# A second buffer of gathered rows, earlier gathers, VectorE low halves and a rewritten start in a chain of four conditioned residual layers

## The reference

```
x = x + L0(x)   # weight of each entry: (cond @ W_dec + b_dec) -> U (256 x 30), U @ V; out = x @ (U V) + bias
x = x + L1(x)   # y = (x * style) @ weight.T * dcoef, clipped to +-256; style, dcoef from cond
x = x + L2(x)   # up(relu(down(x))) + x, with down and up weights scaled and shifted by cond
x = x + L3(x):
    h = ln(x, pw_g[id], pw_b[id]); h = ln(h, cp_g[c], cp_b[c])       # rows gathered by a token id (250) and a class (5)
    t = ln(x, tm_g[c], tm_b[c]);   s = ln(x, ms_g[m], ms_b[m])
    m, n, r = x + mlp_ln(three states of the entry)
    cat = [w0 h, w1 t, w2 m, w3 n, w4 r, w5 s]                        # w = softmax(aw)
    return ln(silu(cat @ W1 + b1) @ W2 + b2) * g + be
```

## Time and profile before

| | us |
|---|---|
| median of 3 runs | 519.87 (519.48 to 520.92) |
| the profiled execution | 522.03 |
| its span, first to last instruction | 520.2 |
| TensorE matmul busy | 486.5 (94%) |
| VectorE busy | 411.8 (79%) |
| GpSimd busy | 406.3 (78%) |
| ScalarE busy | 356.9 (69%) |
| mean granted clock of TensorE | 0.988 |

### The profile page before, as it was taken

One profiled execution on the slowest core, in us unless ns is written; L12 is line 12 of the kernel. 1 busy time (PEld: TensorE's weight loads), 2 busy tenths in 40 slices (PEclk: granted clock), 3 DMA queues, 4 the chain that ended last, 5 costly groups with the idle time before them and its releaser, 6 DMA issues.

```text
span 520.2 us, 9616 instructions
## 1 busy us (share of the span) xinstructions
PE 486.5 (94%) x3216; PEld 360.9 (69%) x3245; DVE 411.8 (79%) x701; ACT 356.9 (69%) x667; POOL 406.3 (78%) x380
## 2 busy tenths in 40 slices
PE   8888598999999999999999999999999999988993
PEld 4854455577768686868686877777777768677782
DVE  4977698678878888878887888787888788887753
ACT  4679557547667777777878777777777776657732
POOL 6737699989787979798888888898989887786501
PEclk9999799999999999999999999999999999999997
DMA  8995507324435171708070717253433424114102
GB/s 302 319 332 108 126 1 219 81 83 93 117 71 137 37 210 30 217 2 241 4 219 28 205 42 186 60 151 96 121 127 89 160 61 134 59 38 126 41 2 80
DMA packets 35118, 61.82 MB, mean 119 GB/s; under 512 B 5108, under 2 KB 17542, under 8 KB 34709
## 3 DMA queue, kind: packets, MB, share of 16 engines
q1 hardware_dynamic: 28788, 44.01, 30.6%
q0 software_dynamic: 5440, 16.87, 11.2%
q10 hardware_dynamic: 864, 0.61, 0.4%
HBM read 52.61 MB, written 8.87 MB: 118 GB/s over the span
## 4 chain that ended last, share of the span: by engine, by line
PE 74%; ACT 8%; DVE 7%; issue 5%; POOL 4%; DMA 1%; DVEq 0%; ACTq 0%; POOLq 0%
PE ps_d L966 10%; PE ps_c L916 9%; PE ps_c L918 9%; PE ps_c L917 9%; PE ps_d L980 5%; PE ps_a L994 4%; PE ps_b L916 3%; PE ps_b L917 3%; PE ps_b L918 3%; PE ps_b L1012 3%; PE ps_a L1006 2%; POOL pw_rows L1532 2%; PE ps_a L1012 2%; DMA set_wdec<-in_W_dec 1%; PE ps_b L935 1%
## 5 line engine op out<-in xcount | busy, mean ns | idle before, releaser
L1232 ACT ACTIVATE h<-h,nb_h,rstd_h 128x256 f32<-128x256 f32 x64 | 33.3, 591 | 41.1 <-POOL nb_h L1562 41.1
L966 PE MATMUL ps_d<-xm_t,l_w 128*128 128x512 f32 x128 | 59.6, 609 | 1.6 <-DVE h L1455 0.9
L1532 POOL DMA_INDIRECT pw_rows<-in_pw,gidx x40 | 39.0, 976 | 12.2 <-issue 12.2
L1577 POOL TENSOR_TENSOR h<-xhat,pw_rows 128x1024 f32<-128x1024 f32 x16 | 38.0, 2372 | 6.4 <-ACT xhat L1232 6.4
L966 PEld LDWEIGHTS ps_d<-xm_t,l_w 128*128 128x128 f32 x128 | 23.5, 193 | 26.6 <-issue 24.5
L1598 POOL TENSOR_TENSOR w_up<-w_up,ugub 128x1024 f32<-128x1024 f32 x16 | 39.0, 2436 | 1.3
L1582 POOL TENSOR_TENSOR h<-h,pw_rows 128x1024 f32<-128x1024 f32 x16 | 38.3, 2394 | 1.2
L1596 POOL TENSOR_TENSOR w_up<-up_rep,ugub 128x1024 f32<-128x1024 f32 x16 | 38.1, 2379 | 1.1 <-issue 0.9
L1608 POOL TENSOR_TENSOR x3be<-x,ln_gb 128x1024 f32<-128x1024 f32 x16 | 37.9, 2371 | 0.6 <-DVE y_out L1513 0.6
L916 PE MATMUL ps_b<-w_h,act_t_l 128*128 128x256 f32 x128 | 37.7, 294 | 0.4 <-DVE act_t_l L1477 0.4
L994 PE MATMUL ps_a<-act_dn,w_up 128*128 128x128 f32 x256 | 32.5, 281 | 5.9 <-ACT act_dn L1211 5.3
(11 more groups left out here) (264 smaller groups left out, 1610.0 us busy)
## 6 DMA issues: line engine op xcount, KB each, us to landing
ugub<-ugub_scratch SPq DMA_DIRECT2D x32, 512.0 KB
x_t<-in_x_t SPq DMA_DIRECT2D x16, 512.0 KB
out<-y_out SPq DMA_DIRECT2D x15, 512.0 KB
set_wdec<-in_W_dec SPq DMA_DIRECT2D x2, 1920.0 KB, 9.9
set_wdec<-in_int_W SPq DMA_DIRECT2D x1, 1536.0 KB, 10.7
set_wdec<-in_nets_rows SPq DMA_DIRECT2D x1, 1152.0 KB, 15.4
set_wdec<-in_nets_W SPq DMA_DIRECT2D x1, 768.0 KB, 6.1
pw_rows<-in_pw,gidx POOLq DMA_INDIRECT x40
```

Of the source, the lines that this page charges most:

```text
L966: m = eng.matmul(ps_l1[:, o, :], l1_w[:, k, o * P:(o + 1) * P], xm_t[:, k, :], start=k == 0, stop=k == KB - 1)
L1232: m = eng.activation(out[:, j, :], src[:, j, :], ACT.Identity, bias=nb[k][:, j:j + 1], scale=rstd[k][:, j:j + 1])
L1532: eng.indirect_dma_start(pw_rows[:, j, :], None, t["pw"], bass.IndirectOffsetOnAxis(ap=idx[:, j:j + 1], axis=0)).then_inc(s_pw[c.ring], 16)
L1577: eng.tensor_tensor(h1[:, :, :], xhat[:, :, :], pw_rows[:, :, 0:D], ALU.mult).then_inc(g_h1m, 1)
```

## The change

- `pw_rows` becomes two buffers, and `g_gather` of a chunk waits for `g_hadd` of two chunks before instead of one. The gather of chunk 1 is issued right behind that of chunk 0.
- `y_out` becomes one buffer instead of two; the last two chunks write into `xm_t` and `x1_even`, which are free by then. `store` stands earlier in SyncE's lists (lag 5, ahead of `load_up`, instead of 6 behind it).
- `act_th2` signals its first strip by itself (`a_th` counts 3 a chunk, not 2), and `g_tlow` waits for that one.
- The four low halves of the weights are made by VectorE: `v_w2low`, `v_w1xlow`, `v_w1tlow`, `v_w1mlow`.
- `act_u` of chunk 0 goes in two halves. Several tiles of the start lie in tiles of later stages, to make room.
- `WARM` goes from 77 matmuls in seven places to 45 in six, and the begin lists of all engines are rewritten. The loop's lists and the end lists of TensorE, ScalarE, VectorE and GpSimd stay as they were.

```diff
-        pw_rows = sb("pw_rows", [P, CT, 2 * D])
+        pw_rows = [sb(f"pw_rows{r}", [P, CT, 2 * D]) for r in range(2)]
...
-        y_out = [late(f"y_out{r}", [P, CT, D]) for r in range(2)]
+        y_out = late("y_out", [P, CT, D])
...
+        y_late = {NCH - 2: rows_in(xm_t), NCH - 1: rows_in(x1_even)}
...
-        WARM = ((z_pool, 1, ps_b, 0, 24), (c_ug, 1, ps_d, 0, 17), (v_dca, 1, ps_a, 0, 8), (v_row, 1, ps_c, 0, 5),
-                (v_cls, 1, ps_c, 1, 2), (v_row, 1, ps_c, 0, 15), (v_ub, 1, ps_b, 1, 6))
+        WARM = ((z_pool, 1, ps_b, 0, 24), (c_ug, 1, ps_d, 0, 10), (v_dca, 1, ps_a, 0, 6), (v_row, 1, ps_c, 0, 1),
+                (v_row, 1, ps_c, 0, 1), (v_ub, 1, ps_b, 1, 3))
...
+        def v_w1xlow(eng, c):
+            eng.wait_ge(c_w1, 2)
+            eng.tensor_tensor(w1_l[:, 4:6, :], w1x[:, :, :], w1_h[:, 4:6, :].bitcast(F32),
+                              ALU.subtract).then_inc(v_wlx, 1)
...
         def act_th2(eng, c):
...
-            wait(eng, a_th, 2 * c.n + 1)
+            wait(eng, a_th, 3 * c.n + 1)
             wait(eng, p_x1, c.n)
-            for lo in (0, RP, 2 * RP):
+            eng.activation(t_st[0:RK, :], t_f, ACT.Copy).then_inc(a_th, 1)
+            for lo in (RP, 2 * RP):
                 m = eng.activation(t_st[lo:lo + RK, :], t_f, ACT.Copy)
             m.then_inc(a_th, 1)
...
         def v_ynorm(eng, c):
...
-            wait(eng, s_store[c.ring], 16 * c.half)
+            if isinstance(c.n, int) and c.n in y_late:
+                wait(eng, p_l1, NCH)
+                wait(eng, v_x3t, NCH - 1)
+            else:
+                wait(eng, s_store[1 - c.ring], 16 * (c.half + c.ring))
...
         def g_gather(eng, c):
...
-            wait(eng, g_h1, c.n)
+            wait(eng, g_h1, c.n - 1)
+            wait(eng, s_pw[c.ring], 16 * CT * c.half)
...
         def g_tlow(eng, c):
-            wait(eng, a_th, 2 * c.n + 2)
+            wait(eng, a_th, 3 * c.n + 2)
...
@@ SyncE @@
-                      order=[(load_ids, 2), (load_shift, 3), (load_x, 0), (load_ub, 0), (load_up, 0), (store, 6)],
+                      order=[(load_ids, 2), (load_shift, 3), (load_x, 0), (load_ub, 0), (store, 5), (load_up, 0)],
...
@@ GpSimd @@
-                      begin=[(g_ones, 0), (g_init, 0), (g_gather, 0), (g_b2rows, 0), (g_tlow, 0), (g_style, 0),
+                      begin=[(g_ones, 0), (g_init, 0), (g_gather, 0), (g_gather, 1), (g_b2rows, 0), (g_tlow, 0),
```

More of the change, by code:

```diff
@@ L251, in conditioned_residuals @@
             ugb = side[:, D + P:D + P + 2 * D]
[L252 to L256, removed]
+            wsq = w_up[:, 0:KB, :]
+            style2 = w_up[:, KB, :].rearrange("p (k b) -> p k b", k=KB)
+            flat_x3 = x3_t[:, :, :].rearrange("p k n -> p (k n)")
+            dm = [flat_x3[:, n * KB * B:(n + 1) * KB * B].rearrange("p (k b) -> p k b", k=KB) for n in range(3)]
+            st_nr = flat_x3[0:64 + 32, 3 * KB * B:3 * KB * B + B]
+            ugub_row = dn_2[:, :, :].rearrange("p a n -> p (a n)")
         nets = ((w1_mem, mu, 0, MU), (w1_nr, st_nr, 0, 64), (w1_nr, st_nr, 64, 96))
@@ L260, in late @@
             return ctx.enter_context(nc.sbuf_tensor(name, shape, dt, side="right"))
-        y_out = [late(f"y_out{r}", [P, CT, D]) for r in range(2)]
+        y_out = late("y_out", [P, CT, D])
+        x3_t_l = late("x3_t_l", [P, KB, CH], F32R)
         act_t_h, act_t_l = (late(f"act_t_{e}", [P, KB, CH], F32R) for e in "hl")
@@ L271, in conditioned_residuals @@
         x3 = late("x3", [P, CT, D])
-        x3_t_h, x3_t_l = (late(f"x3_t_{e}", [P, KB, CH], F32R) for e in "hl")
+        x3_t_h = late("x3_t_h", [P, KB, CH], F32R)
         x1_t = [x1_even, late("x1_odd", [P, KB, CH])]
+        rows_in = lambda tile: tile[:, :, :].rearrange("p k (a d) -> p (k a) d", d=D)
+        y_late = {NCH - 2: rows_in(xm_t), NCH - 1: rows_in(x1_even)}
         x2_t = x1_t
@@ L402, in split_in_place, with y_tile @@
             link(eng.tensor_copy(p3, src))
+        def y_tile(c):
+            return y_late[c.n] if isinstance(c.n, int) and c.n in y_late else y_out
         v_link = chain(nc.vector, v_chain)
@@ L949, in pe_x1 @@
                 eng.wait_ge(c_v, 2)
-            wait(eng, a_th, 2 * c.n + 2)
+            wait(eng, a_th, 3 * c.n + 3)
             wait(eng, g_tl, c.n + 1)
@@ L1070, in pe_hht @@
             if ahead(c, 3):
-                wait(eng, a_th, 2 * (c.n + 3) + 1)
+                wait(eng, a_th, 3 * (c.n + 3) + 1)
             wait(eng, v_h, c.n + 1)
@@ L1270, in act_msh @@
                 eng.wait_ge(v_w1x, 1)
[L1271 to L1272 removed]
+                eng.wait_ge(v_wlt, 1)
+                eng.wait_ge(v_wlm, 1)
             wait(eng, v_ms, c.n + 1)
@@ L1330, in act_store @@
             eng.wait_ge(e_y, 2)
-            eng.dma_start(one(out_d, c)[:, KB:CT - 1], y_out[c.ring][:, KB:CT - 1, :]).then_inc(s_last, 16)
+            eng.dma_start(one(out_d, c)[:, KB:CT - 1], y_tile(c)[:, KB:CT - 1, :]).then_inc(s_last, 16)
         def act_ysquare(eng, c):
@@ L1354, in act_onehot @@
             wait(eng, s_idx[c.ring], 32 * (c.half + 1))
+            wait(eng, a_oh, c.n)
             eng.activation(oh_sq[:, :], idx_ch[c.ring][:, :], ACT.Square, bias=cls_neg[RP:RP + CLS, 0:1]).then_inc(a_sq, 1)
@@ L1576, in g_hmul @@
             wait(eng, p_hht, c.n)
-            eng.tensor_tensor(h1[:, :, :], xhat[:, :, :], pw_rows[:, :, 0:D], ALU.mult).then_inc(g_h1m, 1)
+            eng.tensor_tensor(h1[:, :, :], xhat[:, :, :], pw_rows[c.ring][:, :, 0:D], ALU.mult).then_inc(g_h1m, 1)
         def g_hadd(eng, c):
             eng.wait_ge(g_h1m, c.n + 1)
-            eng.tensor_tensor(h1[:, :, :], h1[:, :, :], pw_rows[:, :, D:2 * D], ALU.add).then_inc(g_h1, 1)
+            eng.tensor_tensor(h1[:, :, :], h1[:, :, :], pw_rows[c.ring][:, :, D:2 * D], ALU.add).then_inc(g_h1, 1)
         def g_rooth(eng, c):
```

152 lines of the change are left out of this document (76 added, 76 removed).

## The result

The changed kernel takes **525.15 us** (median of 5 runs, 523.9 to 526.52); the kernel before, beside it, 520.92 (5 runs, 519.48 to 521.75). The ratio is 1.0086 (95% interval 1.0064 to 1.0108): 0.9% slower where 0.6% faster was forecast. The profiled execution took 526.52 us, span 524.7, mean granted clock 0.976 (before 0.988).

The account below looks back on a forecast made before the run. TensorE was taken to bound 160 to 400, untouched by the change; nearly 33 of the first 100 us were waiting or filling. Start gains carried to -2.9 at l1 of chunk 4, loop and end 0: 519.87 - 2.9 = 517.0, range 513.5 to 520.6.

Parts of the forecast that it names:

- step 1: Start, t of chunk 0: second gather pushes b2's rows to 33.3; t's low half starts 1.1 us later, absorbed.
- step 6: Clock at the start: full at the first up product; lower at the second, after some 6 us waiting, costing 0.9 us.
- step 9: Loop and end: 0 us from the earlier t signal, single y_out, last chunks' own tiles and moved store.
- 2: ScalarE's tables at the start: a 1.28 us load goes; the second-layer product starts at 42.5 instead of 43.33.
- 3: Chunk 0's down product: w1sum leaves the front of its scaling; dn ready at 49.8, 5.4 us earlier.
- 4: Chunk 0's up product: early gather delays ugub 3.6 us to 48.3; product starts at 53.2, 3.1 us earlier.
- 5: VectorE, x3's sum of chunk 0 to chunk 1's: 22.9 us of work; second up product at 78.5, 1.8 us earlier.
- VectorE as the bound: Rival, 0.20, about the same: three low halves before x2 of chunk 2 wait up to 7.2 us for GpSimd; 519.3.
- 7: Loop start: low halves on VectorE, gather gone there; root of chunk 1 at 87.4, loop at 97.0, 3.2 us earlier.
- 8: First two slots: root x of chunk 2 at 115.0, 0.9 us earlier; l1 of chunk 4 at 139.3, 2.9 earlier.
- the rival of the clock: Rival, 0.13, slower: TensorE waits three times at the start; two low-clock stretches cost 6.6 us, giving 523.6.

Follow-up runs that it names:

- e5: A with the second gather's four issues moved on GpSimd from ahead of b2's rows to behind the mem root; 523.58 us, ratio 1.0049.
- e7: A with the edits of both e5 and e6 (second gather later, four fills in GpSimd's setup); 521.21 us, ratio 1.0011.
- e11: B with w1sum behind the mixer outputs' norm, and W1's high-half copies and two of GpSimd's low halves moved too; 523.41 us, ratio 1.0027.
- B: The kernel before the change; 520.92 us beside the changed kernel.
- e8: e7 with 27 warming matmuls ahead of the second up product (chunk 1); 521.65 us, ratio 0.9996.
- e9: e8 with w2's centring, dcoef's first step, x1's sum and dcoef's reciprocal ahead of the gains on VectorE; 520.25 us, ratio 0.9947.
- e12: e9 with the third gather behind chunk 0's residual on GpSimd instead of ahead of chunk 2's root; 519.35 us, ratio 0.9988.
- e13: e7 with the third gather behind chunk 0's residual on GpSimd instead of ahead of chunk 2's root; 519.96 us, ratio 0.9995.
- e14: The same kernel as e9, run again beside e12 and e13; 517.59 us, ratio 0.9954 against B.
- A: The changed kernel, with the whole change against B; 525.15 us, ratio 1.0086.
- a0: Control: A unaltered, run again; 525.53 us, ratio 1.0112.
- e6: A with four small fills added to GpSimd's setup; 522.55 us, ratio 1.0035.
- e10: The same kernel as e3, run later on another chip; 529.72 us, ratio 1.0146.
- e15: A with four small fills behind GpSimd's last root; 528.26 us, ratio 1.0139.
- e1: A with 35 instead of 10 warming matmuls ahead of dcoef's products; 532.47 us, ratio 1.0171.
- e2: e1 with 27 warming matmuls more ahead of the second up product; 527.74 us, ratio 1.0124.
- e3: A with b2's rows moved on GpSimd from ahead of t's low half of chunk 0 to behind style of chunk 1; 531.48 us, ratio 1.0184.
- e16: A with eight small fills added to GpSimd's setup; 528.65 us, ratio 1.0152.

## Why the prediction was wrong, by its steps

Three steps failed: step 1 called the lateness of t's low half absorbed, step 6 priced the clock at 0.9 us at one place, and step 9 put the end at 0. What the other steps put between these places came out in its lengths, only later.

- **1, t of c0, failed.** b2's rows began at 28.65 as said, but took 6.2 us for 4.7 and ended at 34.8, not 33.3: those that ran while VectorE picked the gains (28.74 to 32.66) were longer (one cast took 1.00 for 0.39). So t's low half began 2.6 late instead of 1.1. And it was not absorbed: TensorE waited 5.62 us, with only 10 of the 17 warming matmuls left, so l1's product ended at 47.2 for 42.0. e5 and e7 show that the second gather's place costs 1.3 to 2 us of the total. In both the clock still fell at l1 of c0 (6.2 and 5.3 us); x1's sum waited behind the gains there.
- **2 and 3.** One of four table loads went, but the hidden layer's product came behind the late l1, at 47.0. w1sum took 0.68 and 0.69 at its new place, as said. dn was ready at 54.7, not 49.8, because x2 was 4.6 late. In e11, where it is not, dn is ready at 50.6, 4.6 us before B's 55.2 (5.4 said), and the up product starts at 53.0: the step was right but for 0.8 us, its start time wrong.
- **4 held in its times, and its reason isn't shown.** ugub of c0 let w_up begin at 47.48 (48.3 said), w_up ended at 52.3 (53.1 said); only the down part came later than both. The step blamed the second gather's megabyte for 3.6 us of it. But e7, which issues that gather only behind the mem root, waits for ugub just as long:

```profile
47.40 2.37 POOL L1620 TENSOR_TENSOR w_up<-up_rep,ugub 128x1024 f32<-128x1024 f32 x1 [4.39 <-DMA ugub<-ugub_scratch]
```

Over the profiles w_up begins at 44.4 to 48.3 with four gather issues before 35 us (e5, e7, e8, e9, e12, e13, e14) and at 47.5 to 50.1 with eight and no late signal there (A, a0, e6, e10, e15). That is some 2 us by the middles, with a spread of 3 to 4 within each, and 44.7 without the gather was an estimate.
- **5 held in its durations** (W1's first low half 1.08, where I took 0.6 and 0.45 of waiting; the tm and h part 1.22, the ms part 0.69 and W2's 0.66, where I took 1.2, 0.6, 0.6), not in its start. From x3's sum of c0 to dn of c1 it was 22.3 us (57.88 to 80.16), where 55.3 to 77.5 is 22.2; the step's own terms, 55.3 + 22.9 - 1.2, give 77.0. VectorE as the bound (0.20) is refuted as that rival put it: no low half took over 1.3 us.
- **6, the clock, failed: it was sized for one place, and it fell at three.** Said: full clock at the first up product (right), 0.9 us at the second. Measured: 1.9 on l1 of c0, 1.7 on the second up product (2.1 with what follows, e7 against e8), and some 1.6 at the end of the loop. It fell before 70, which the prediction had named as a sign of being wrong.
- **7 and 8** hung on 5's lead: root x of c1 at 91.8 for 87.4, loop start at 101.45 for 97.0, l1 of c4 at 143.98 for 139.3. In 8 the order was as said, but x1 of c3 came so late that root x of c2, behind style and gather, stood at 119.3 for 115.0.
- **9, "loop and end: 0", failed at the end.** Stores and y_out cost nothing, as said: in e6, which has them, the stretch to the end is 378.1 as in B. The slots kept 27.2 us. But 2.7 us went at the loop's exit, from one instruction that nothing in the profile of before could show: with the four low halves gone, four instructions fewer stand ahead of it on GpSimd.

The result is nearest the rival of the clock (0.13, 523.6), and its picture of the start is right. It is no hit all the same: of the 4.2 us lost, the runs give 2.5 to 2.7 to the loop's exit, which no rival had, and 1.3 to 2 to the second gather's place. That its number is within 1.6 us of the measured 525.15 is in good part luck. The kernel with four further edits (the second gather elsewhere, four instructions on GpSimd, a cover of the second gap and another order on VectorE) is faster than B by 0.46%, 2.4 us (e14). That is near the 2.9 I had forecast, but it isn't the forecast come true: with the first two edits the kernel was only level, the cover by itself shows nothing clear in a total, and the order on VectorE was no part of the sum.

Open: what late signals are. Before 35 us they stand in 4 of 9 profiles with eight gather issues there (e1, e2, e3, e16) and in 1 of 10 with four (e9); at ScalarE's read near 115 in 8 of 14 with the third gather issued beside it and in 0 of 5 without. That fits a link with gathers and doesn't show one; e7 and e14 have that gather there and no late signal. The chip is a rival that the runs don't exclude: on the chip of a0, e5, e6 and e7 no profile has one, and e3, e15 and e16, on two others, were 6 to 10 us above B's median in every run. The chip alone doesn't settle it either, as e9 and e14 ran on one. Why a place in GpSimd's program makes an instruction slow was not shown either.

## What to carry to other kernels

Work moved ahead of a critical instruction on an in-order engine isn't absorbed because something else was late before: price the gap that it opens, and the clock behind that gap, at each place where the other engine then waits. A gain at one place counts only at the next place where the same engine waits; read such places apart, as start, loop and end. When an engine's program gains or loses instructions, compare also the places the change never touched: if one instruction has become longer there, try a few cheap instructions in the setup; here four brought it back.

## What was unexpected of the hardware

- One gather issue took 1.92 us for 0.95, in every one of eight profiles with the same number of GpSimd instructions ahead of it, and in none of eleven with four or eight more. The Trainium skill ("Runtime: NRT & Kernel Launch", Instruction fetch mechanics) says that engines fetch their program in blocks and that crossing into the next is mostly hidden. The traces agree that loading goes in blocks: the packets of the instruction queues are of 8 and 16 KB, and one of 8 KB starts 2.5 to 3.7 us before each slow issue. No run here shows that fetching is what took the time; if it is, it was not hidden at that place, and cost 1.0 us and, with the clock, 2.7.
- An engine may begin 2 to 4 us after the TensorE product it waits for has ended, with no releaser on the core, in some executions of a kernel and not in others (e9: 6.5 us in all, e14: none).
- After A's waits of 5.62 and 6.14 us the granted clock was 0.50, the lower of its two levels (1.2 GHz): l1's product took 5.57 us for 3.67, the up product 3.75 for 2.02. A wait of 1.84 to 1.87 us at the loop's exit was followed by the lower level in three profiles of eight, and by none in the other five; one of 0.87 to 0.89 us by none in eleven.
